# Row sums for the input's norm, inverse roots spread by transfers, and another order on ScalarE

## The chip, the core and the metric

The program runs on one core of a Trainium2 chip, in one launch. The metric is the device time of that launch in microseconds (us). The core has a matrix engine (TensorE, "PE" in the profile, its weight loads "PEld"), three engines for elementwise work (VectorE "DVE", ScalarE "ACT", GpSimd "POOL"), and SyncE ("SP"), which here issues all transfers. The engines run their own instruction streams and meet at semaphores. Data lie in SBUF (128 partitions), matmuls write to PSUM banks, and larger data lie in the chip's memory (HBM).

## The reference

Two transformer layers over x of shape (16, 256, 256): 16 batch entries, 256 positions, 256 features. Layer 0, cut to what matters:

```python
def _tc_rmsnorm(x, t, gw, gb, bw, bb):
    g = (t @ gw.T + gb)[:, None, :]
    b = (t @ bw.T + bb)[:, None, :]
    inv_rms = jax.lax.rsqrt(jnp.mean(x * x, axis=-1, keepdims=True) + EPS)
    return g * x * inv_rms + b
# layer 0 (inside), with 16 heads of 16
z = x + _attention(_tc_rmsnorm(x, t, g1w, g1b, b1w, b1b), Wq, Wk, Wv, Wo)
y0 = z + _swiglu(_tc_rmsnorm(z, t, g2w, g2b, b2w, b2b), gate_w, hid_w, out_w)   # hidden size 1024
x1 = x + y0
# layer 1: masked attention of x1, then
out = out @ Wo.T
rms = jnp.sqrt(jnp.mean(out * out, axis=-1, keepdims=True) + EPS)
xn = out / rms * rms_scale
xn = xn * (1.0 + sc[:, None, :]) + shift[:, None, :]
result = x1 + xn
```

So there are three norms with a root per position: of the input (layer 0 only, "N"), of the attention's output with the residual (layer 0, "C"), and of the attention's output (layer 1, "C" and then "R"). The mask keeps the first so many key positions for all rows. In layer 1 the kernel takes a short path in which one half of the keys is skipped; the profiled execution takes it.

## The kernel before

Everything is kept transposed: features on partitions, positions along the free dimension, so a batch entry is a tile of 128 x (2 x 256). Matrix products are made of three matmuls on split operands (a high part and a low part, `mm3`, lines 525 to 527), which is why so many "high" and "low" tiles appear.

The work is a pipeline over 32 items: 16 batch entries in layer 0 and the same 16 in layer 1. A step s works on several items at once (`stages`): N of item s+3 (its norm and split), A of s+2 (Q and K projections), V and B1 of s+1 (value projection; scores for the row maxima), B2 of s (scores again, exponentials, half of the value product), C of s-1 (second half of the value product, division, output projection, squares for the norm), C2/C3 of s-2 and s-3 (SwiGLU, layer 0 only), R of s-2 (layer 1's norm applied and stored). Steps run from -3 to 33. Steps 2 to 12 have all of layer 0's stages, 13 to 16 have no N of layer 0 any more, 17 is the passage, and 18 to 29 are layer 1's; steps 30 to 33 empty the pipeline. Each step has eight slots g = 0..7, and the order on every engine is written out by hand: each engine's `step` walks the slots and issues its work there. No scheduler moves anything.

Two PSUM banks (`work0`, `work1`) are handed out in turn to all uses named in `bank_uses`: T1a, T1b, sh1, Q, T2, Wo, K, V, ms, sh0, F0 to F7, bcC, bcN. A use waits until the use two places before it in the list has been read. From step 19 on the small uses sh0, sh1 and bcR have a third bank, `acc`.

A norm before the change goes like this. Squares: on GpSimd, `nrm<-X` for the input in slot 2 (line 1280) and `dg<-y` for the output in slot 3 (line 1294). Mean squares: on TensorE with a column of 1/256 (`mean_squares`, line 710), slot 5 in layer 0, slot 6 in layer 1, into the bank "ms". VectorE adds epsilon (`rsqrt`, line 938), GpSimd raises to -0.5 (`inverse_roots`, line 1261). VectorE multiplies the roots into identity matrices (`diagonals`, line 945), TensorE multiplies these by ones, which puts the root of each position in every partition (`broadcast_rstd`, line 718; uses bcC, bcN in slot 6, bcR in slot 1 of the next step). VectorE then multiplies (`normalize`, line 951), reading the roots from PSUM. ScalarE applies gain and shift per partition (`affine`, line 1084) and casts the high part; GpSimd subtracts for the low part (`xnl`, line 1322, or `xcl`, line 1314), and TensorE's projections (Q and K of the next step wait for `n_lo`) or the SwiGLU's first product (waits for `c_lo`) use them. In slot 7 of layer 0 the output's affine pair and its cast stand on ScalarE ahead of the slot's exponentials `E<-s2ps` (line 1055), and the value product (`values`, line 622) at the next step's start waits for these.

Q and K are split in three bf16 parts: high on ScalarE, the rest on VectorE (`rest`, line 919), middle on ScalarE (`middle`, line 1102), low on GpSimd (line 1233). SyncE writes the parts to a scratch tensor (`scr<-qp`, `scr<-kp`, line 412) and reads them back stacked along partitions (`read_stack`, line 422, `stack<-scr`), 768 KB per half of the heads; the scores of the next step read the stack. The attention's output is transposed in slot 2 (T2, line 670), ScalarE casts its high part (`oh`, line 1115), VectorE makes the low part (`ol`, line 909), and slot 3's output projection multiplies them.

SyncE's queue is in program order too: the x load, the shift rows of half 1, the writes of Q and K, `read_stack` of half 0, the store of a result (layer 1), the shift rows of half 0, `read_stack` of half 1. A wait in it holds everything behind it.

At the start, GpSimd also sets constant rows of the stacks (`stack_constants`, six memsets), in slot 3 of the first step, and SyncE loads the weights, 1 MB each.

## Time and profile before

| | us |
|---|---|
| median of 3 runs | 1011.88 |
| lowest, highest | 1011.34, 1016.07 |
| the profiled execution, its own time | 1008.46 |
| its span, first to last instruction | 1006.6 |
| TensorE busy | 909.2 (90%) |
| VectorE busy | 570.3 (57%) |
| ScalarE busy | 547.5 (54%) |
| GpSimd busy | 415.2 (41%) |
| transfers, mean share of the 16 engines | 39.8% |

The busy shares are means over very different stretches. The start, until about 100 us, fills the pipeline; layer 0 runs until about 740 us, with one full step every 39.6 us; layer 1 runs to about 960; the rest empties the pipeline. The 40 slices of the page show TensorE at nine tenths or more from slice 5 to slice 29 and at eight in layer 1; transfers take two to three tenths in layer 0 and five to seven in layer 1. A timeline row gives the start, the length, the engine, the line and the operation; what is in brackets at its end is the idle time before it and the instruction whose end ended it. A matmul group's length holds a modelled tail of about 0.16 that overlaps with the next group.

### The profile page before, as it was taken

The page shows a single profiled execution, that of the slowest core. Times are in us where ns is not written, and L with a number is a line of the kernel's source. Part 1 is how long each engine was busy: PE and PEld are TensorE (multiplying, and loading weights), DVE is VectorE, ACT ScalarE, POOL GpSimd, SP SyncE. Part 2 cuts the span into 40 slices and gives each one's busy share as a digit, 9 for nine tenths or more (in the row PEclk, how much of TensorE's full clock was granted, in tenths as well). Part 3 has the DMA queues.
Part 4 walks back from the last instruction along what each step waited for, and adds up shares of the span by engine and source line. Part 5 has one row for each costly group of instructions (what it writes and reads, how often), then busy time and mean ns, then how long its engine had stood idle before and what let it go on. Part 6 is the DMA issues. An engine that isn't in the chain of part 4 may idle for free.

```text
span 1006.6 us, 24326 instructions
## 1 busy us (share of the span) xinstructions
PE 909.2 (90%) x8188; PEld 780.6 (78%) x8188; DVE 570.3 (57%) x1104; ACT 547.5 (54%) x1130; POOL 415.2 (41%) x633
## 2 busy tenths in 40 slices
PE   3578899999999999999999999999999789888874
PEld 3456698898888988988889889889887677777653
DVE  3366556557555565575565756545455455555541
ACT  2246556546455565464554665554556566666652
POOL 5223344443443444434334344344444454444522
PEclk9779999999999999999999999999999999999997
DMA  6555423322332233223322242232437576576611
GB/s 204 110 106 122 91 64 75 75 65 59 66 86 42 63 73 73 63 58 68 84 42 63 69 91 65 65 76 66 94 74 167 119 160 147 142 166 144 157 36 34
DMA packets 83070, 91.29 MB, mean 91 GB/s; under 512 B 7776, under 2 KB 70016, under 8 KB 83008
## 3 DMA queue, kind: packets, MB, share of 16 engines
q1 hardware_dynamic: 83008, 90.50, 39.8%
q8 instruction: 35, 0.57, 0.3%
q14 instruction: 27, 0.22, 0.1%
HBM read 60.30 MB, written 29.36 MB: 89 GB/s over the span
## 4 chain that ended last, share of the span: by engine, by line
PE 73%; issue 8%; DVE 7%; ACT 5%; POOL 3%; DMA 1%; SPq 1%; POOLq 0%; DVEq 0%; ACTq 0%
PE work L525 11%; PE work L527 11%; PE work L526 11%; PE pvps L622 8%; PE s2ps L606 7%; PE s1ps L583 5%; PE work L710 4%; PE acc L525 3%; PE acc L526 2%; PE acc L527 2%; PE work L656 2%; PE s1ps L568 2%; PE work L718 1%; DVE rest L919 1%; DVE th L959 1%
## 5 line engine op out<-in xcount | busy, mean ns | idle before, releaser
L1055 ACT ACTIVATE E<-s2ps 128x512 f32<-128x512 f32 x384 | 214.1, 596 | 184.2 <-PE s2ps L606 110.8
L882 DVE TENSOR_REDUCE nmax<-s1ps 128x2 f32<-128x512 f32 x256 | 163.9, 682 | 32.1 <-PE s1ps L583 31.9
L525 PE MATMUL work<-xch,Gh 128*128 128x256 f32 x512 | 154.5, 302 | 0.0
L959 DVE SCALAR_TENSOR_TENSOR th<-th,work 128x256 f32<-128x256 f32 x128 | 53.8, 420 | 168.7 <-ACT th L1073 168.7
L1328 POOL TENSOR_TENSOR hl<-hf,hh 128x256 fp32r<-128x256 f32 x128 | 94.9, 742 | 131.0 <-PE acc L527 77.3
L526 PE MATMUL work<-xcl,Gh 128*128 128x256 f32 x512 | 147.1, 287 | 0.0
L527 PE MATMUL work<-xch,Gl 128*128 128x256 f32 x512 | 146.9, 287 | 0.0
L606 PE MATMUL s2ps<-stack 100*128 100x256 bf16 x768 | 127.7, 275 | 2.1 <-DMA stack<-rows 2.0
L875 DVE TENSOR_REDUCE nmax<-s1ps 128x4 f32<-128x512 f32 x128 | 85.6, 685 | 36.5 <-PE s1ps L568 36.4
L525 PEld LDWEIGHTS work<-xch,Gh 128*128 128x128 f32 x512 | 99.3, 194 | 8.2 <-issue 6.6
L622 PE MATMUL pvps<-E,vaug 128*32 128x256 f32 x1536 | 97.5, 387 | 6.3 <-ACT E L1055 4.0
L1233 POOL TENSOR_TENSOR qp<-rest,qp 128x512 bf16<-128x512 f32 x32 | 37.2, 1163 | 156.3 <-ACT qp L1102 156.3
L527 PEld LDWEIGHTS work<-xch,Gl 128*128 128x128 f32 x512 | 100.0, 195 | 0.0
L526 PEld LDWEIGHTS work<-xcl,Gh 128*128 128x128 f32 x512 | 99.9, 195 | 0.0
L583 PE MATMUL s1ps<-stack 96*128 96x256 bf16 x512 | 81.9, 281 | 9.4 <-DMA stack<-scr 4.9
L1073 ACT ACTIVATE th<-work 128x256 f32<-128x256 f32 x128 | 49.1, 384 | 72.3 <-PE work L527 72.3
L525 PE MATMUL work<-xnh,Wh 128*128 128x256 f32 x256 | 79.3, 310 | 1.4 <-issue 0.8
L606 PEld LDWEIGHTS s2ps<-stack 100*128 100x128 bf16 x768 | 67.3, 98 | 14.1 <-issue 2.3
L622 PEld LDWEIGHTS pvps<-E,vaug 128*32 128x32 f32 x1536 | 43.8, 110 | 40.3 <-issue 9.5
L525 PE MATMUL acc<-hh,Uh 128*128 128x256 f32 x256 | 74.2, 290 | 0.2
L526 PE MATMUL work<-xnl,Wh 128*128 128x256 f32 x256 | 74.4, 291 | 0.0
L527 PE MATMUL work<-xnh,Wl 128*128 128x256 f32 x256 | 74.2, 290 | 0.0
(131 smaller groups left out, 2149.1 us busy)
## 6 DMA issues: line engine op xcount, KB each, us to landing
stack<-scr SPq DMA_DIRECT2D x64, 384.0 KB, 4.6
stack<-scr SPq DMA_DIRECT2D x64, 256.0 KB, 5.2
scr<-qp SPq DMA_DIRECT2D x64, 192.0 KB, 2.3
scr<-kp SPq DMA_DIRECT2D x64, 192.0 KB, 2.3
stack<-scr SPq DMA_DIRECT2D x64, 128.0 KB, 5.6
X<-xT SPq DMA_DIRECT2D x16, 256.0 KB, 4.5
yT<-crm SPq DMA_DIRECT2D x16, 256.0 KB, 5.2
stack<-rows SPq DMA_DIRECT2D x196, 4.0 KB
```

Of the source, the lines that this page charges most:

```text
L525: mm(out, lh, rh, start=first, stop=False, skip_group_check=True)
L526: mm(out, lh, rl, start=False, stop=False, skip_group_check=True)
L527: return mm(out, ll, rh, start=False, stop=last, skip_group_check=True)
L583: last = mm(bank[:, T * i:T * (i + 1)], qst[par][0:PARTS, h, P * qh:P * (qh + 1)], kst[par][0:PARTS, h, :], start=st.L["B1"] == 0, stop=Tr ...
L606: last = mm(bank[:, T * i:T * (i + 1)], kst[par][0:ROWS, h, P * kh:P * (kh + 1)], qst[par][0:ROWS, h, :], start=not add_mask, stop=True, s ...
L622: last = mm(pvps[32 * i:32 * (i + 1), T * (j % 2):T * (j % 2 + 1)], v_of[:, kh, h, :], E[:, exp_slot(layer, st.full, h // 2, kh), T * (h % ...
L875: v.tensor_reduce(nmax[:, g // 4, :, 2 * (g % 4):2 * (g % 4) + 2], s1ps[g % 2][:, :].rearrange("p (q h t) -> p q h t", q=2, h=2), AX_X, AL ...
L882: v.tensor_reduce(nmax[:, g // 4, qh, 2 * (g % 4):2 * (g % 4) + 2], s1ps[u % 2][:, :].rearrange("p (h t) -> p h t", h=2), AX_X, ALU.max, n ...
L959: v.scalar_tensor_tensor(th[:, i % 2, :], th[:, i % 2, :], 1.0, bank[:, 0:T], ALU.add, ALU.mult).then_inc(silu_ready, 1)
L1055: a.activation(E[:, exp_slot(st.L["B2"], st.full, g, kh), :], s2ps[g % 2 if short else u % 2][:, :], ACT.Exp, scale=SCORE_SCALE).then_inc( ...
L1073: a.activation(th[:, i % 2, :], bank[:, 0:T], ACT.Tanh, scale=0.5).then_inc(tanh_ready, 1)
L1328: p.tensor_tensor(hl[:, i % 2, :], hf[:, i % 2, :], hh[:, i % 2, :].bitcast(F32), ALU.subtract).then_inc(h_low, 1)
```

## The change

It does five things.

1. Input's norm: the row sums. The input is also given by rows (`x_rows`: positions on partitions). SyncE loads that tile into `nrm`, ScalarE squares it in slot 3 with a scale of 1/16, and VectorE sums it along the free dimension. GpSimd's squares and TensorE's mean squares of the input go.
2. The slot. In steps with layer-0 work, `mean_squares` (output only), the variances and the roots are in slot 4 (was 5). In layer 1 they stay in slot 6.
3. Spreading. `diagonals` and `broadcast_rstd` go, with the bank uses bcR, bcC and bcN. SyncE writes the 2 or 4 roots of each partition to a small tensor in HBM, waits for the landing, and reads the whole of it back into every partition of `dg`. In layer-0 steps this stands behind `read_stack` of half 0 and ahead of the shift rows of half 0; in layer 1 behind these rows and ahead of `read_stack` of half 1. `normalize_c` and `normalize_n` read `dg` with a step of 4 or 2 elements.
4. ScalarE in layer-1 steps: the middle part of K moves from the end of slot 1 to slot 2, behind `oh` and the slot's exponentials.
5. The start: the input rows are the first load; ScalarE waits for the conditioning (`cond_ready`) only in slot 7 of the first step; GpSimd's `stack_constants` move from slot 3 to the first step's end, behind `xnl`.

```diff
-        return 5
+        return 4
     return None if L["C"] is None else 6
+def norm_columns(L):
+    return 0 if L["N"] == 0 else 2, 4 if L["C"] is not None else 2
...
-        if g == 1 and L["R"] is not None:
-            uses.append("bcR")
-        if g == 6:
-            uses += ["bcC"] * (L["C"] == 0) + ["bcN"] * (L["N"] == 0)
...
+        r_scr = nc.dram_tensor("r_scr", (P, 4), F32, kind="Internal").ap()
...
+            def load_rows(n):
+                sp.dma_start(flat(nrm[:, :, :]), x_rows[:, bass.ds(n * TC * D, TC * D)]).then_inc(rows_loaded, 16)
+            load_rows(0)
             load_x(0)
...
+                def spread_roots():
+                    c0, c1 = norm_columns(L)
+                    after(sp, rstd_spread, spread_before)
+                    after(sp, rstd_ready, roots_made)
+                    k = c1 - c0
+                    sp.dma_start(bass.AP(r_scr.tensor, 0, [[k, P], [1, k]]), rstd[:, c0:c1]).then_inc(rstd_written, 16)
+                    after(sp, rstd_written, roots_written)
+                    sp.dma_start(flat(dg[:, c0:c1, :]),
+                                 bass.AP(r_scr.tensor, 0, [[0, P], [1, k * P]])).then_inc(rstd_spread, 16)
...
                 if L["B2"] is not None:
                     rows_in(1)
+                if L["N"] == 0 and st.s0 > FIRST:
+                    after(sp, n_lo, split_before)
+                    load_rows(n_x)
...
                 load_swap(6)
+                if norm_slot(L) == 4:
+                    spread_roots()
                 if L["R"] is not None:
                     store_result(st.n(-2 - B), result_made)
                 if L["B1"] is not None:
                     rows_in(0)
+                if norm_slot(L) == 6:
+                    spread_roots()
...
-                if st.L["N"] == 0:
-                    after(pe, sq_n, st.n(3) + 1)
-                    jobs.append((nrm[:, :, :], 0))
...
-            def broadcast_rstd(st, use, col):
-                bank, full = open_bank(st, use)
-                after(pe, diag_ready, st.n(2 if use == "bcR" else 3) + 1)
-                mm(bank[:, 0:T], ones[:, :], dg[:, col:col + 2, :].rearrange("p a b -> p (a b)"),
-                   start=True, stop=True).then_inc(full, 1)
...
+            def variances(st):
+                if st.L["N"] == 0:
+                    n = st.n(3)
+                    after(dve, sq_n, n + 1)
+                    v.tensor_reduce(sums[:, :], nrm[:, :, :], AX_X, ALU.add).then_inc(sums_ready, 1)
+                    after(dve, sums_ready, n + 1)
+                    v.tensor_scalar(var[:, 0:2], sums[:, :], EPS, VAR_TOP, ALU.add, ALU.min).then_inc(var_ready, 1)
+                if st.L["C"] is not None:
+                    bank, free = opened(st, "ms")
+                    v.tensor_scalar(var[:, 2:4], bank[:, 0:2], EPS, VAR_TOP, ALU.add, ALU.min).then_inc(free, 1)
+            def spread(made, col):
+                c0, c1 = norm_columns(made.L)
+                after(dve, rstd_spread, 16 * (made.n(3) + 1))
+                by_row = flat(dg[:, c0:c1, :]).rearrange("q (p c) -> q c p", c=c1 - c0)
+                return by_row[:, col - c0:col - c0 + 2, :][:, None, :, :].to_broadcast([P, FC, TC, P])
+            def normalize_c(made):
+                v.tensor_tensor(halves(crm[:, :, :]), halves(y[:, :, :]), spread(made, 2), ALU.mult).then_inc(c_normed, 1)
...
+                    if g == 2 and L["A"] == 1:
+                        middle(st, "K", kp, k_mid)
                     if g == 2 and L["R"] is not None:
...
+                    if g == 3 and L["N"] == 0:
+                        n = st.n(3)
+                        after(act, rows_loaded, 16 * (n + 1))
+                        a.activation(nrm[:, :, :], nrm[:, :, :], ACT.Square, scale=D ** -0.5).then_inc(sq_n, 1)
...
-                    if g == q_slot(L, 1):
+                    if g == 2 and L["A"] == 0:
                         middle(st, "K", kp, k_mid)
...
-                    if g == 3 and st.s0 == FIRST:
-                        pool.wait_ge(sq_n, 1)
-                        for i in range(2):
-                            stack_constants(i)
-                        pool.wait_ge(stack_ones, 6)
...
+                if st.s0 == FIRST:
+                    pool.wait_ge(n_lo, 1)
+                    for i in range(2):
+                        stack_constants(i)
+                    pool.wait_ge(stack_ones, 6)
```

GpSimd's queue in the first two steps, before (`xnl` is the input's low part, `qp` and `kp` the low parts of Q and K, line 1280 the input's squares):

```order
16 L1280 TENSOR_TENSOR nrm<-X 128x512
17 L1225 MEMSET stack 4x2048
18 L1226 MEMSET stack 1x2048
19 L1228 MEMSET stack 1x2048
20 L1225 MEMSET stack 4x2048
21 L1226 MEMSET stack 1x2048
22 L1228 MEMSET stack 1x2048
23 L1261 TENSOR_TENSOR rstd<-var,power 128x2
24 L1322 TENSOR_TENSOR xnl<-nrm,xnh 128x512
25 L1233 TENSOR_TENSOR qp<-rest,qp 128x512
```

and the same place after the change:

```order
16 L1280 TENSOR_TENSOR rstd<-var,power 128x2
17 L1328 TENSOR_TENSOR xnl<-nrm,xnh 128x512
18 L1240 MEMSET stack 4x2048
19 L1241 MEMSET stack 1x2048
20 L1243 MEMSET stack 1x2048
21 L1240 MEMSET stack 4x2048
22 L1241 MEMSET stack 1x2048
23 L1243 MEMSET stack 1x2048
24 L1248 TENSOR_TENSOR qp<-rest,qp 128x512
25 L1248 TENSOR_TENSOR kp<-rest,kp 128x512
```

The memsets stood ahead of the roots and now stand between `xnl` and the first Q's low part.

ScalarE's queue in a layer-1 step, slots 1 to 3, before (`kp<-work` is K's high part, `kp<-rest` its middle part, `oh` the output's high part):

```order
775 L1146 CAST kp<-work 128x512
776 L1102 CAST kp<-rest 128x512
777 L198 REGISTER_ALU
778 L1115 CAST oh<-work 128x512
779 L198 REGISTER_ALU
780 L1055 ACTIVATE E<-s2ps 128x512
```

and after:

```order
780 L1156 CAST kp<-work 128x512
781 L1126 CAST oh<-work 128x512
782 L199 REGISTER_ALU
783 L1068 ACTIVATE E<-s2ps 128x512
784 L199 REGISTER_ALU
785 L1068 ACTIVATE E<-s2ps 128x512
786 L1115 CAST kp<-rest 128x512
```

The middle part moved behind `oh` and the exponentials; of the two rows of exponentials there, an execution on the short path runs one.

TensorE's queue between slot 6 and slot 7 of a full layer-0 step, before (`acc` is the SwiGLU's second product):

```order
931 L527 MATMUL acc<-hh,Ul 128x256
932 L198 REGISTER_ALU
933 L718 MATMUL work<-dg,ones 128x256 x2
934 L198 REGISTER_ALU
935 L583 MATMUL s1ps<-stack 128x256 x2
```

and after:

```order
915 L556 MATMUL acc<-hh,Ul 128x256
916 L199 REGISTER_ALU
917 L612 MATMUL s1ps<-stack 128x256 x2
```

The two broadcasts between them are gone.

## Rows read from the trace of the kernel before

**Rows 1.** stages by window: us, then busy (xinstructions) of each engine, clock, DMA.

```profile
200.00:300.00 100.00, 98.59 (x886) 88.44 (x888) 62.87 (x120) 52.81 (x115) 40.62 (x59) 0.98 0.30 67
800.00:900.00 100.00, 88.12 (x866) 71.75 (x865) 55.44 (x112) 66.09 (x127) 48.28 (x79) 0.98 0.65 146
```

**Rows 2.** TensorE's timeline, one layer-0 step: start us, us, engine, line, operation [idle before].

```profile
423.15 0.95 PE L710 MATMUL work<-mean,nrm 128*128 128x1 f32 x8
...
432.05 0.70 PE L718 MATMUL work<-dg,ones 128*128 128x256 f32 x2 [0.23 <-DVE hf L963]
...
435.71 0.64 PE L622 MATMUL pvps<-E,vaug 128*32 128x256 f32 x8
```

**Rows 3.** ScalarE's timeline, the same stretch.

```profile
432.78 1.09 ACT L1084 ACTIVATE crm<-crm,cond 128x256 f32<-128x256 f32 x2 [1.41 <-DVE crm L951]
...
434.43 1.08 ACT L1055 ACTIVATE E<-s2ps 128x512 f32<-128x512 f32 x2
```

**Rows 4.** VectorE's timeline, the same stretch.

```profile
431.91 0.68 DVE L951 TENSOR_TENSOR crm<-y,work 128x512 f32<-128x512 f32 x1
```

**Rows 5.** GpSimd's timeline, the same stretch.

```profile
431.45 0.73 POOL L1328 TENSOR_TENSOR hl<-hf,hh 128x256 fp32r<-128x256 f32 x1 [2.27 <-PE acc L527]
```

**Rows 6.** VectorE's timeline at 758 us.

```profile
758.57 0.42 DVE L945 TENSOR_TENSOR dg<-ident,rstd 128x256 f32<-128x256 f32 x1
```

**Rows 7.** GpSimd's timeline at 758 us.

```profile
758.74 0.33 POOL L1247 TENSOR_TENSOR nparts<-nmax,units 128x16 bf16<-128x16 f32 x1 [0.94 <-DVE nmax L889]
759.14 0.22 POOL L1249 TENSOR_TENSOR nrest<-nmax,nparts 128x16 f32<-128x16 f32 x1
```

**Rows 8.** VectorE's timeline, a layer-1 step at 855 us.

```profile
854.97 0.69 DVE L919 TENSOR_TENSOR rest<-work,kp 128x512 f32<-128x512 f32 x1 [1.38 <-ACT kp L1146]
856.90 0.69 DVE L909 TENSOR_TENSOR ol<-work,oh 128x512 fp32r<-128x512 f32 x1 [1.24 <-ACT oh L1115]
```

**Rows 9.** ScalarE's timeline, the same stretch.

```profile
855.69 0.62 ACT L1102 CAST kp<-rest 128x512 bf16<-128x512 f32 x1 [0.81 <-DVE rest L919]
856.21 0.58 ACT L1115 CAST oh<-work 128x512 fp32r<-128x512 f32 x1
```

**Rows 10.** TensorE's timeline in layer 1.

```profile
857.64 0.38 PE L525 MATMUL work<-oh,Wh 128*128 128x256 f32 x1 [1.63 <-DVE ol L909]
...
879.12 0.40 PE L568 MATMUL s1ps<-stack 97*128 97x128 bf16 x4
```

**Rows 11.** SyncE's DMA issues in layer 1.

```profile
867.38 1.38 SPq L422 DMA_DIRECT2D stack<-scr  x3
```

**Rows 12.** GpSimd's timeline at the start.

```profile
4.62 1.80 POOL L1225 MEMSET stack<- 4x2048 f32 x1
...
13.38 1.80 POOL L1228 MEMSET stack<- 1x2048 f32 x1
...
25.06 1.26 POOL L1322 TENSOR_TENSOR xnl<-nrm,xnh 128x512 fp32r<-128x512 f32 x1 [8.32 <-ACT xnh L1179]
31.47 1.16 POOL L1233 TENSOR_TENSOR qp<-rest,qp 128x512 bf16<-128x512 f32 x1 [5.15 <-ACT qp L1102]
```

**Rows 13.** TensorE's timeline at the start.

```profile
44.87 1.04 PE L583 MATMUL s1ps<-stack 96*128 96x256 bf16 x4 [4.90 <-DMA stack<-scr]
...
47.12 0.56 PE L525 MATMUL work<-xnh,Wh 128*128 128x256 f32 x1
```

**Rows 14.** time to landing of the transfers that L385 issues.

```profile
DMA to landing us min/median/max: 2.7/4.5/8.7
```

**Rows 15.** time to landing of the transfers that L412 issues.

```profile
DMA to landing us min/median/max: 2.1/2.3/4.6
```

**Rows 16.** GpSimd's and VectorE's timeline at the end.

```profile
997.78 0.71 POOL L1261 TENSOR_TENSOR rstd<-var,power 128x2 f32<-128x2 f32 x1 [1.45 <-DVE var L938]
...
1000.39 0.69 DVE L951 TENSOR_TENSOR crm<-y,acc 128x512 f32<-128x512 f32 x1 [1.44 <-PE acc L718]
```

More of the change, by code:

```diff
@@ L141, in turns_of @@
     uses = bank_uses(stages(s))
-    small = [u for u in uses if s >= SPARE and u in ("sh0", "sh1", "bcR")]
+    small = [u for u in uses if s >= SPARE and u in ("sh0", "sh1")]
     return [u for u in uses if u not in small], small
@@ L763, in step @@
                             divide_out(st)
-                    if g == ms_slot(L):
+                    if g == norm_slot(L) and L["C"] is not None:
                         mean_squares(st)
@@ L1256, in inverse_roots @@
             def inverse_roots(st):
[L1258 to L1260 removed]
+                c = slice(*norm_columns(st.L))
+                if st.L["N"] == 0:
+                    after(pool, var_ready, st.n(3) + 1)
+                if st.L["C"] is not None:
+                    b, k = st.bank("ms")
+                    after(pool, work_free[b], k + 1)
+                after(pool, rstd_written, 16 * st.n(3))
                 p.tensor_tensor(rstd[:, c], var[:, c], power[:, c], ALU.pow).then_inc(rstd_ready, 1)
@@ L1289, in step @@
                         after(pool, work_free[b], k + 1)
-                        b, k = st.bank("bcR") if L["R"] is not None else \
-                            st.last().bank("bcN" if st.last().L["N"] == 0 else "bcC")
-                        after(pool, work_full[b], k + 1)
+                        after(pool, c_normed, st.n(-1))
                         p.tensor_tensor(dg[:, :, :].rearrange("p (c u) t -> p c (u t)", c=FC),
```

103 lines of the change are left out of this document (36 added, 67 removed).

## The prediction

> **What bounds the kernel now.** I read the stages by window first, then each engine's timeline through one step of each kind, then the start and the end. In layer 0's steady part TensorE is busy 98.6 of 100 us, so an instruction taken from it is time, provided nobody else becomes late. In layer 1 it is busy 88.1 of 100 us, so there a chain with gaps sets the pace [rows 1]. The gap is one wait per step: TensorE stands 1.63 us in front of the output projection, for `ol` [rows 10]. In the first 100 us the pipeline is filling: every step waits for a chain through several engines, and nothing hides an added transfer. So I price the start, the eleven full layer-0 steps, the twelve layer-1 steps and the end apart. I price the four mixed steps between (13 to 16) in a sentence.
>
> **Layer 0, steps 2 to 12.** The mean squares of the input leave TensorE: 0.84 us, half of the block whose first half starts at 423.15 and reads 0.95 with its modelled end [rows 2]. The two broadcasts leave too. The second starts at 432.05 after waiting for VectorE to free its bank, and lasts 0.70 with its tail [rows 2]. Together with the first one and that wait TensorE would be free about 1.4 us earlier in slot 7. Most of that is not to be had. Its next long work, the value product at 435.71 [rows 2], needs the last exponentials. These stand on ScalarE behind the two affine instructions of the output's norm (432.78) and a cast, and end at 434.43 + 1.08 = 435.51 [rows 3]. That chain hangs on VectorE's normalize at 431.91 [rows 4], which program order puts behind the sixth slot's SwiGLU, and none of it used the removed matmuls in a way that delays it. So the broadcasts give only the slack 435.71 - 435.51 = 0.20. Sum so far: 0.84 + 0.20 = 1.04 per step.
>
> What hides the replacement: the mean squares move a slot forward, where the squares are ready over a microsecond earlier. ScalarE's square (about 0.6, as a cast of 512 columns, 0.62 in [rows 9]) and VectorE's sum (0.68, as any 512-column pass, [rows 4]) fall into idle time ahead of slot 4's work. The roots are then ready about 5 us earlier than now, and two transfers of 2.3 us [rows 15] fit ahead of 431.9. I cost them at nothing; without the cover it would be up to 4.6.
>
> Two things make the normalize itself later, and it is on the chain. First, its multiplier now comes from SBUF, not PSUM, so it reads two SBUF operands. The trace shows what such an instruction does to GpSimd: while VectorE's `dg<-ident,rstd`, also with two SBUF operands, runs from 758.57 to 758.99 [rows 6], GpSimd's first shift operation, started at 758.74, takes 0.33 and ends 0.08 after it, while its sister takes 0.22 [rows 7]. I take this as one waiting for the other. In the layer-0 step GpSimd's `hl` runs from 431.45 to 432.18 [rows 5], across 431.91, so the normalize starts 0.27 later. The Trainium skill (SBUF — State Buffer, Summary: rules for kernel authors) says that when VectorE has two SBUF inputs and GpSimd reads SBUF, the second to issue is fully blocked; by that rule, the trace agrees.
>
> Second, with four roots per row the multiplier is read with a step of 16 bytes. No row shows such a read. The bounds are 0.68, the present duration at unit step [rows 4], and twice that, 1.36, if each element took two turns. I take 0.98, so 0.30 more, with 0 and 0.68 kept for the range. Per step: 1.04 - 0.27 - 0.30 = 0.47; eleven steps give 5.2 us (bounds 1.0 and 8.5). The four mixed steps lose a broadcast, keep the slack of 0.20 each, and have only two roots per row: 0.8 us.
>
> **Layer 1, steps 18 to 29.** ScalarE now does the middle part of K (855.69, 0.62), then `oh` (856.21, 0.58) [rows 9]; VectorE's `ol` follows at 856.90 and TensorE at 857.64 [rows 8, 10]. With `oh` first it runs directly after the high part of K, ends near 855.5, and what is late next is VectorE itself: K's rest ends at 854.97 + 0.69 = 855.66 [rows 8], and `ol` starts behind it at 855.6. That is 1.3 earlier. TensorE must have the transposed output ready for this; it comes earlier too, as the broadcast that stood ahead of it is gone. Twelve steps: 15.6 us. The middle part of K slips by about 0.2 behind `oh` and one exponential, so GpSimd's low part, the K write and the stack read slip with it, and the step is shorter by 1.3. I take the first half of the stack read as still hidden. The roots' round trip sits on SyncE's queue ahead of the second half of the stack read (867.38 [rows 11]) and holds it for the write's landing, 2.3 [rows 15], and an issue of 0.4. Its last part is issued at 868.76 now and lands some 4.5 later, as a 256 KB load does [rows 14], at 873.3; it is needed at 879.12 [rows 10]. The 5.8 in hand become 5.8 - 2.7 - 1.3 = 1.8. So it costs nothing; rival 3 has the price if that fails.
>
> **The start.** Six memsets of the stacks, now from 4.62 to 15.18 in GpSimd's idle time [rows 12], move behind the first low part `xnl`. They last 13.38 + 1.80 - 4.62 = 10.56. `xnl` ends at 26.32 now [rows 12] and some 0.8 later then (one more load in front, one round trip behind a 1 MB load). So the memsets end near 37.7, and Q's low part, at 31.47 now [rows 12], is 6.2 late. K's low part follows it, then K's write and the stack read: the first scores move from 44.87 [rows 13] to 51.1. Worse, SyncE issues the roots' write behind that read. The queue serves in order as far as the trace tells: a 256 KB load lands in 4.5 as a rule and 8.7 behind two stack reads [rows 14]. So the roots are written at about 51.4, and read back 2.3 later [rows 15] at 53.8. From normalize to `xnl` it takes 0.7 + 1.1 + 0.6 + 1.3 and some hand-overs, 57.8. The next Q projection starts there instead of at 47.12 [rows 13]: +10.7. The next two steps put the roots' write behind a stack read again, at (8.7 - 4.5) / 2 = 2.1 each [rows 14]. Together 14.9 us later. Bounds: 8 if small writes overtake the stack reads, 17 if each round trip takes the longest landing.
>
> **The end.** The last group's roots (997.78 + 0.71 = 998.49) reach normalize at 1000.39 now, 1.9 later [rows 16]; with two transfers of 2.3 [rows 15] it is 4.7 later, so +2.8. Steps 30 and 31 save the 1.3 of the layer-1 step each: -2.6. Sum +0.2.
>
> **Sum.** 14.9 - 5.2 - 0.8 - 15.6 + 0.2 = -6.5 us. The profiled execution took 1008.46 us (span 1006.6), so 1002.0 by its own measure. The median of the runs, 1011.88, lies 3.4 above it: 1005.4.
>
> **Rivals.**
> 1. The start is cheap. If the small write overtakes the bulk reads, the start costs 8 and the sum is -13.4: 998.5. For it: the write is 128 tiny rows over all 16 engines. Against it: the 8.7 of [rows 14].
> 2. The strided read costs double, 1.36, on the chain of each of the eleven steps. Layer 0 then gives 1.04 - 0.27 - 0.68 = 0.09 per step, 1.0 us in all instead of 5.2: 1009.6, no change. For it: nothing in the rows has this step; against it: all rows of 512 columns on VectorE take 0.68 to 0.69, whatever they read. The Trainium skill (SBUF — State Buffer, Door 1: The DMA port swizzle) says that full rate needs two hits in a 16-byte line, and names four fp32 as the step that is still free. This read sits on that edge: one sentence of the page makes it slower, the other does not, and no row here decides.
> 3. Slower: the round trip turns layer 1 into a transfer-bound chain. SyncE waits on the roots' write before it may issue the second half of the stack read. If the write lands like the slowest of [rows 15], in 4.6, and the read-back ahead of that half takes another 1.6 from it, it is 2.3 + 1.6 = 3.9 later than I have it, with 1.8 in hand: twelve steps stand 2.1 us each in front of slot 4's scores, 25.2 us: 1005.4 + 25.2 = 1030.6. It decides from a landing of 2.3 + 1.8 = 4.1 us on. For it: transfers take 0.65 of the engines' time in layer 1 [rows 1]. Against it: at 867.38 the queue has just drained, and the medians are 2.3.
>
> **How the numbers follow.** Chances: forecast 0.42, rival 1 0.20, rival 2 0.26, rival 3 0.12. About 0.5% (5 us) is what a measurement can tell from no change. The forecast's own range, 999 to 1011, lies below 1006.8 in about 0.6 of cases and within 0.5% otherwise; rival 1 is faster; rival 2 is faster in 0.2, else the same, rarely slower; rival 3 is slower. Faster 0.42 x 0.62 + 0.20 + 0.26 x 0.2 = 0.51; slower 0.12 + 0.02 = 0.14; same 0.35. The range takes in rival 1 with a little more gain and rival 2 with the long start: 995 to 1015.
>
> **What would show it.** In layer 0 the normalize of the output (`crm<-y,dg`) shows the read's price, 0.68, 0.98 or 1.36, and TensorE an idle stretch of about a microsecond in front of the value product of the next step, released by the exponentials. In layer 1 TensorE's wait for `ol` falls from 1.63 to about 1, and the step is 1.3 shorter. The first Q projection after the first scores stands near 58 and the scores themselves near 51. Wrong would be: first scores still near 45 (the memsets don't hold Q's low part), TensorE waiting for `stack` in slot 4 of layer 1, or the broadcasts' full 1.4 us gained per layer-0 step, which would mean that the exponentials came earlier by another way.

## The result and the profile after

The changed kernel takes 1080.47 us (median of 4 runs, 1078.02 to 1082.12) against 1012.17 for the kernel before: 1.0665 times as long, 95% interval 1.0627 to 1.0702. I had predicted 1005.4. The profiled execution took 1082.12, its span is 1080.3.

The chain that ended last names the new thing at once (shares of the span, by engine and then by line):

```profile
PE 49%; DMA 17%; issue 14%; POOL 6%; ACT 5%; DVE 4%; SPq 4%; ACTq 0%; POOLq 0%; DVEq 0%
PE work L554 7%; PE work L556 7%; PE work L555 7%; PE pvps L651 6%; PE s2ps L635 5%; DMA stack<-rows 5%; DMA r_scr<-rstd 5%; PE s1ps L612 4%; DMA dg<-r_scr 3%; DMA stack<-scr 2%; PE work L733 2%; DMA scr<-kp 2%; PE work L685 2%; DVE crm L963 2%; PE acc L554 2%
```

Transfers hold 17% of it, the two of the round trip (`r_scr<-rstd`, `dg<-r_scr`) 8%. The windows of [rows 1], after the change (us, then busy of each engine, clock, DMA share):

```profile
200.00:300.00 100.00, 95.83 (x890) 86.41 (x889) 64.34 (x122) 55.99 (x123) 40.24 (x59) 1.00 0.38 85
800.00:900.00 100.00, 79.37 (x741) 64.28 (x740) 46.14 (x91) 56.01 (x108) 42.50 (x70) 0.91 0.64 139
```

Shares don't say where 74 us of span are. A ledger does: I took the start of one instruction that every step has, ScalarE's cast of K's high part, and subtracted (all in us; the last column is my forecast).

| stretch | before | after | change | forecast |
|---|---|---|---|---|
| start to K of step 2 | 129.8 | 166.8 | +37.0 | +14.9 |
| step 2 to 13 | 443.3 | 430.9 | -12.4 | -5.2 |
| 13 to 18 | 173.2 | 185.1 | +11.9 | -0.8 |
| 18 to 29 | 196.3 | 223.2 | +26.9 | -15.6 |
| 29 to the end | 64.0 | 74.3 | +10.3 | +0.2 |

**The start.** The chain of waits from 46 to 65 us (start, length, what), which answers to [rows 12, 13]:

```profile
46.40 2.33 DMA scr<-kp
...
50.17 5.15 DMA r_scr<-rstd
55.34 5.82 DMA dg<-r_scr
61.25 0.70 DVE nrm L967
...
65.11 0.58 PE work L554
```

A 1 KB write and its 128 KB read-back take 11.0 us. I had the write 0.3 behind the landing of the stack read and the read-back at 2.3. The first scores stand at 54.96, the Q projection behind them at 65.11. The two landings by stretch (median): in full layer-0 steps, where they are 2 KB and 256 KB, 2.4 and 3.2, in steps 13 to 16 3.3 and 4.1, in the start 5.1 and 4.0 (up to 6.6 and 5.8), in layer 1 4.5 and 5.1.

**Layer 0.** VectorE, ScalarE's exponentials and TensorE around the normalize, as in [rows 2 to 4]:

```profile
422.63 1.23 DVE L963 TENSOR_TENSOR crm<-y,dg 128x512 f32<-128x512 f32 x1
423.78 1.10 DVE L967 TENSOR_TENSOR nrm<-X,dg 128x512 f32<-128x512 f32 x1
...
425.70 1.08 ACT L1068 ACTIVATE E<-s2ps 128x512 f32<-128x512 f32 x2
...
426.90 1.93 PE L651 MATMUL pvps<-E,vaug 128*32 128x256 f32 x32 [1.76 <-ACT E L1068]
```

The value product waits 1.76 us for the exponentials, which hang on a normalize of 1.23 instead of 0.68. The period is 39.19 us; before it was 39.6 in six steps and 41.1 in five. In each of those five the granted clock is 0.96, so mostly 2.4 GHz and for a part of the time 1.2; after the change all eleven have 1.00. One of the five and one of the six, both of the kernel before:

```profile
248.70:289.90 41.20, 40.65 (x360) 36.41 (x358) 24.92 (x48) 22.06 (x49) 16.71 (x25) 0.96 0.30 65
331.00:370.60 39.60, 39.06 (x358) 34.83 (x357) 24.73 (x48) 21.91 (x49) 16.61 (x25) 1.00 0.32 67
```

TensorE's rows of the first one show where the clock falls:

```profile
262.54 1.03 PE L710 MATMUL work<-mean,dg 128*128 128x1 f32 x8
...
265.01 0.41 PE L527 MATMUL work<-xch,Gl 128*128 128x256 f32 x1
265.22 0.41 PE L525 MATMUL work<-xch,Gh 128*128 128x256 f32 x1
```

These matmuls start 0.21 apart, and from 268.1 on 0.12 again. In all five steps the fall comes 1.0 to 1.5 us behind the end of the sixteen 128x1 matmuls of the mean squares. The other six steps have the same sixteen and no fall.

**Steps 13 to 17.** Two rows of TensorE and one of GpSimd:

```profile
625.18 1.93 PE L651 MATMUL pvps<-E,vaug 128*32 128x256 f32 x32 [2.47 <-ACT E L1068]
...
641.13 0.39 PE L554 MATMUL acc<-hh,Uh 128*128 128x256 f32 x1 [1.96 <-POOL hl L1339]
```
```profile
639.24 1.15 POOL L1248 TENSOR_TENSOR kp<-rest,kp 128x512 bf16<-128x512 f32 x1 [7.55 <-ACT kp L1115]
```

In the first the round trip is late for the normalize. The second is new too: `hl` stands behind K's low part on GpSimd, and K's middle part moved behind the exponentials already in step 14, since Q and K of steps 14 to 17 belong to layer 1.

**Layer 1.** TensorE's waits of [rows 10] and SyncE's queue of [rows 11]:

```profile
920.13 0.39 PE L597 MATMUL s1ps<-stack 97*128 97x128 bf16 x4 [1.13 <-DMA stack<-scr]
923.11 0.39 PE L635 MATMUL s2ps<-stack 100*128 100x256 bf16 x2 [2.59 <-DMA stack<-rows]
...
930.22 0.39 PE L554 MATMUL work<-oh,Wh 128*128 128x256 f32 x1 [0.73 <-DVE ol L918]
```
```profile
913.33 1.27 SPq L432 DMA_DIRECT2D stack<-scr  x3
914.81 0.40 SPq L437 DMA_DIRECT2D yT<-crm  x1
915.32 2.04 SPq L481 DMA_DIRECT2D stack<-rows  x3
917.46 0.38 SPq L489 DMA_DIRECT2D r_scr<-rstd  x1
923.19 0.34 SPq L491 DMA_DIRECT2D dg<-r_scr  x1
923.57 1.38 SPq L432 DMA_DIRECT2D stack<-scr  x3
```

The wait for `ol` fell from 1.63 to 0.73, where I had named about 1. In its place are two waits for transfers, and SyncE issues the read-back 5.7 us behind the write, for whose landing it waits.

### The profile page after: what moved, and what is told of

It reads as the page before. It is cut to its first block, busy times and chain, and to the rows that moved or that the text cites. A ratio compares the mean times of both kernels' runs of the same rounds, so it can differ in the third digit from the quotient of the medians.

```text
span 1080.3 us, 23966 instructions
## 1 busy us (share of the span) xinstructions
PE 885.6 (82%) x7964; PEld 756.2 (70%) x7964; DVE 576.3 (53%) x1096; ACT 552.7 (51%) x1146; POOL 400.0 (37%) x617
## 4 chain that ended last, share of the span: by engine, by line
PE 49%; DMA 17%; issue 14%; POOL 6%; ACT 5%; DVE 4%; SPq 4%; ACTq 0%; POOLq 0%; DVEq 0%
PE work L554 7%; PE work L556 7%; PE work L555 7%; PE pvps L651 6%; PE s2ps L635 5%; DMA stack<-rows 5%; DMA r_scr<-rstd 5%; PE s1ps L612 4%; DMA dg<-r_scr 3%; DMA stack<-scr 2%; PE work L733 2%; DMA scr<-kp 2%; PE work L685 2%; DVE crm L963 2%; PE acc L554 2%
## 5 line engine op out<-in xcount | busy, mean ns | idle before, releaser
L635 PE MATMUL s2ps<-stack 100*128 100x256 bf16 x768 | 131.9, 281 | 19.5 <-DMA stack<-rows 18.8
L555 PE MATMUL work<-xcl,Gh 128*128 128x256 f32 x512 | 144.7, 283 | 0.0
L556 PE MATMUL work<-xch,Gl 128*128 128x256 f32 x512 | 144.4, 282 | 0.0
L976 DVE SCALAR_TENSOR_TENSOR th<-th,work 128x256 f32<-128x256 f32 x128 | 53.9, 421 | 168.1 <-ACT th L1086 168.0
L651 PE MATMUL pvps<-E,vaug 128*32 128x256 f32 x1536 | 100.0, 395 | 34.8 <-ACT E L1068 28.6
L612 PE MATMUL s1ps<-stack 96*128 96x256 bf16 x512 | 84.5, 286 | 45.1 <-DVE nmax L891 26.1
L556 PEld LDWEIGHTS work<-xch,Gl 128*128 128x128 f32 x512 | 97.5, 190 | 0.0
L555 PEld LDWEIGHTS work<-xcl,Gh 128*128 128x128 f32 x512 | 97.5, 190 | 0.0
L612 PEld LDWEIGHTS s1ps<-stack 96*128 96x128 bf16 x512 | 43.5, 102 | 66.7 <-issue 22.2
L554 PE MATMUL work<-xnh,Wh 128*128 128x256 f32 x256 | 82.9, 324 | 2.7 <-POOL xnl L1328 2.2
L1248 POOL TENSOR_TENSOR kp<-rest,kp 128x512 bf16<-128x512 f32 x32 | 40.4, 1262 | 120.2 <-ACT kp L1115 120.2
```

Source lines behind the costliest of these rows:

```text
L554: mm(out, lh, rh, start=first, stop=False, skip_group_check=True)
L555: mm(out, lh, rl, start=False, stop=False, skip_group_check=True)
L556: return mm(out, ll, rh, start=False, stop=last, skip_group_check=True)
L612: last = mm(bank[:, T * i:T * (i + 1)], qst[par][0:PARTS, h, P * qh:P * (qh + 1)], kst[par][0:PARTS, h, :], start=st.L["B1"] == 0, stop=Tr ...
L635: last = mm(bank[:, T * i:T * (i + 1)], kst[par][0:ROWS, h, P * kh:P * (kh + 1)], qst[par][0:ROWS, h, :], start=not add_mask, stop=True, s ...
L651: last = mm(pvps[32 * i:32 * (i + 1), T * (j % 2):T * (j % 2 + 1)], v_of[:, kh, h, :], E[:, exp_slot(layer, st.full, h // 2, kh), T * (h % ...
```

## The experiments

My first reading was that SyncE's wait for this landing makes layer 1 slow (rival 3 of the prediction), that the queue order makes the round trip slow at the start, and that part 4 gains a little. The kernels below went against most of that. Spans by the stretches of the ledger, us, one profiled execution each:

| kernel | to step 2 | 2-13 | 13-18 | 18-29 | rest | ratio to before (95%) |
|---|---|---|---|---|---|---|
| before | 129.8 | 443.3 | 173.2 | 196.3 | 64.0 | |
| after | 166.8 | 430.9 | 185.1 | 223.2 | 74.3 | 1.0665 (1.0627-1.0702) |
| mid_only | 132.0 | 443.2 | 182.0 | 213.8 | 69.0 | 1.0262 (1.0217-1.0308) |
| diag | 134.5 | 426.1 | 181.0 | 208.8 | 65.5 | 1.0104 (1.0063-1.0145) |
| late_read | 166.9 | 430.9 | 184.5 | 229.8 | 72.9 | 1.0635 (1.0588-1.0682) |
| consts_first | 162.7 | 430.9 | 186.4 | 223.0 | 76.8 | 1.0656 (1.0605-1.0708) |
| store_late | 130.5 | 443.2 | 182.0 | 192.9 | 67.2 | 1.0069 (1.0036-1.0102) |
| sums_only | 127.9 | 426.0 | 173.8 | 197.9 | 65.8 | 0.9788 (0.9739-0.9837) |
| spread_early | 161.5 | 430.9 | 185.8 | 222.8 | 74.3 | 1.0632 (1.0578-1.0685) |
| pool_write | 160.9 | 431.0 | 186.8 | 224.6 | 79.2 | 1.0665 (1.0611-1.0720) |
| thin_read | 168.0 | 430.9 | 185.0 | 214.2 | 73.3 | 1.0563 (1.0534-1.0591) |
| sums_store | 131.0 | 426.1 | 173.8 | 193.2 | 63.8 | 0.9781 (0.9748-0.9814) |
| sums_best | 128.3 | 426.1 | 173.8 | 190.9 | 63.7 | 0.9750 (0.9727-0.9772) |
| unit_step | 168.1 | 426.5 | 187.0 | 223.7 | 75.8 | 1.0665 (1.0590-1.0740) |

Kernels with the same instructions in a stretch agree there within 0.1 us in steps 2 to 13, but within some 3 us in the start and 5 in layer 1. So I read the small effects from the stretch or the step that they belong to.

### mid_only

```diff
+                    if g == 2 and L["A"] == 1:
+                        middle(st, "K", kp, k_mid)
...
-                    if g == q_slot(L, 1):
+                    if g == 2 and L["A"] == 0:
                         middle(st, "K", kp, k_mid)
```

> The kernel before with part 4 alone: K's middle part behind the output's high part and the exponentials, in every step whose Q and K projections belong to layer 1 (14 to 29). Theory: two effects. In the layer-1 steps TensorE's wait for ol falls from 1.63 to 0.7, as in the changed kernel's trace, so 12 x 0.9 = 11 us less. In steps 14 to 17 K's low part comes later and GpSimd's hl stands behind it; in the changed kernel TensorE waits 1.96, 1.98, 1.61 and 1.61 us there, so 7 us more. Sum -4: 1008. Rival A (the recorded prediction): only the gain, 1.3 per step, 996.6. Rival B: part 4 is what slows layer 1, 27 us more: above 1030.

1041.95 us: rival B. TensorE waits 1.95, 2.00, 1.62 and 1.61 for `hl` in steps 14 to 17, as in the changed kernel, and layer 1 takes 17.5 us more though the wait for `ol` is down to 0.5 per step. Its waits in layer 1, 780 to 960 us (total, times, longest), of before and of mid_only:

```profile
PE work L525 <- DVE ol L909: 16.0, 10, 1.6
...
PE s2ps L606 <- DMA stack<-rows: 1.7, 2, 1.5
PE s1ps L568 <- DMA stack<-scr: 1.2, 1, 1.2
```
```profile
PE s2ps L606 <- DMA stack<-rows: 12.1, 9, 1.6
PE s1ps L568 <- DMA stack<-scr: 5.4, 8, 0.8
PE work L525 <- DVE ol L909: 4.9, 9, 0.6
```

SyncE's queue tells why. First before, where the output projection of this step starts at 876.15, then mid_only, where it starts at 857.43:

```profile
876.14 0.89 SPq L412 DMA_DIRECT2D scr<-kp  x2
878.94 1.27 SPq L422 DMA_DIRECT2D stack<-scr  x3
880.42 0.41 SPq L427 DMA_DIRECT2D yT<-crm  x1
882.41 2.06 SPq L469 DMA_DIRECT2D stack<-rows  x3
```
```profile
858.93 0.89 SPq L412 DMA_DIRECT2D scr<-kp  x2
861.71 1.27 SPq L422 DMA_DIRECT2D stack<-scr  x3
863.20 0.41 SPq L427 DMA_DIRECT2D yT<-crm  x1
863.71 2.06 SPq L469 DMA_DIRECT2D stack<-rows  x3
```
```profile
868.26 0.39 PE L568 MATMUL s1ps<-stack 97*128 97x128 bf16 x4 [0.79 <-DMA stack<-scr]
869.97 0.39 PE L606 MATMUL s2ps<-stack 100*128 100x256 bf16 x2 [1.31 <-DMA stack<-rows]
```

Measured from the output projection, the first half of the stack read was issued at +2.8 and is now at +4.3, since TensorE has come nearer to K, not K to TensorE. It lands at +10.8, 6.55 after its issue, and TensorE is there 0.79 earlier. The shift rows are issued at +6.3 in both, but now 2.0 us behind the stack read and 0.5 behind the result's store instead of 3.5 and 2.0, and they land at +12.5; before, TensorE used them at +10.2 without a wait. The gain of 1.1 at `ol` is repaid by 2.1 in front of transfers. The granted clock falls with it, from 0.98 to 0.93 in 800:900, that is, more of this stretch runs at 1.2 instead of 2.4 GHz: after the waits of this step the projections' matmuls start 0.21 apart, elsewhere 0.12. Steps 18 to 29, before and in mid_only, show that this is the larger part:

```profile
746.28:942.59 196.31, 171.31 (x1701) 139.08 (x1700) 110.56 (x221) 127.08 (x242) 92.24 (x154) 0.99 0.66 149
757.28:971.10 213.82, 183.13 (x1701) 149.13 (x1700) 111.60 (x221) 127.05 (x243) 92.10 (x154) 0.93 0.60 137
```

The same 1701 matmuls keep TensorE busy for 11.8 us more, and it is idle for 5.7 more.

### diag

Part 3 undone: `diagonals`, `broadcast_rstd` and the uses bcR, bcC, bcN are back, `spread_roots` goes. All else stays as in the changed kernel.

> The changed kernel with part 3 undone: the roots go through identity matrices and a matmul with ones again (bank uses bcC, bcN, bcR), all the other parts stay. Theory: the spreading by transfers is nearly all of the 68 us. What stays is the memsets' shift at the start (+5.6, K's low part 5.6 later by them), 0.84 us less of TensorE per full layer-0 step (-9, and perhaps some us more where the granted clock rises), +7 in steps 14 to 17 and -11 in layer 1: 1012 + 5.6 - 9 + 7 - 11 = 1005, between 998 and 1012. Rival: the parts other than the spreading carry a good part of the loss (row sums behind a later load, part 4 in layer 1): 1030 or more.

1022.54 us. Against the changed kernel the start is 32.3 us shorter, layer 0 4.8, steps 13 to 18 4.1, layer 1 14.4 and the end 8.8: the spreading costs 58 us by the medians (1080.5 - 1022.5), 64 by the two profiled executions (diag's is the fastest of its six runs), and is the main cause. My number was too low, since it had part 4 as a gain; what is left over before, +7.8 in 13 to 18 and +12.5 in layer 1, is mid_only again. A full layer-0 step takes 38.73.

### late_read and thin_read

late_read, in layer-1 steps, and thin_read:

```diff
-                    after(sp, rstd_written, roots_written)
-                    sp.dma_start(flat(dg[:, c0:c1, :]), ...
...
                     read_stack(par, 1)
+                if norm_slot(L) == 6:
+                    read_roots()
```
```diff
-                    sp.dma_start(flat(dg[:, c0:c1, :]),
-                                 bass.AP(r_scr.tensor, 0, [[0, P], [1, k * P]])).then_inc(rstd_spread, 16)
+                    q = 16 if norm_slot(L) == 6 else P
+                    sp.dma_start(flat(dg[0:q, c0:c1, :]),
+                                 bass.AP(r_scr.tensor, 0, [[0, q], [1, k * P]])).then_inc(rstd_spread, 16)
```

> The changed kernel with one move on SyncE's queue, in layer-1 steps only: the wait for the roots' write and the read-back stand behind the second half of the stack read, not ahead of it. Theory: layer 1 is slow because SyncE stands 4.2 us per step (33.9 us in 8 waits) on the landing of a 1 KB write while the stack read waits behind it. Then the 11 steps from 782.7 to 1006.0 (223 us) fall to some 190 to 200, and the kernel to 1050 (1045 to 1058). Rival: the two extra transfers slow the others by sharing the engines, wherever they stand: 1075 to 1082.

> The changed kernel, but in layer-1 steps the roots are read back into 16 of the 128 partitions only (16 KB instead of 128 KB), so layer 1's norm is left out for the others. Theory: GpSimd's own queue and the later read-back did not bring layer 1's 14 us (against diag) back, since they left the volume; with an eighth of it the waits for the stack and the rows fall towards diag's (7.7 and 12.0 in ten steps), and the kernel takes 1068 to 1072. Rival: it is the number of transfers and the landings that count, not the volume: 1078 to 1082.

late_read: 1080.04, the rival. The second half of the stack read is issued 0.4 us behind the roots' write, not 6.1, and nothing comes of it. In steps 18 to 29 TensorE's wait for the stack falls from 16.6 to 11.3 us and its wait for the rows grows from 18.0 to 25.4, so rival 3 of my prediction had the sign right and the mechanism wrong. thin_read, whose layer-1 results are not the norm's: 1069.9, as expected, and layer 1 is 9.0 shorter in the ledger. Over these steps the two waits are 28.0 instead of 34.6 (diag 21.4), and TensorE's matmuls take 3.0 less, at a clock of 0.94 instead of 0.93. So the size of the read-back counts for more than half of the 14.4. Bytes and number of pieces both fell to an eighth, and no run separates them; the other 5 us, as much as the scatter of this stretch, stay open.

### consts_first

```diff
+                    if g == 3 and st.s0 == FIRST:
+                        pool.wait_ge(consts, 5)
+                        for i in range(2):
+                            stack_constants(i)
+                        pool.wait_ge(stack_ones, 6)
```

> The changed kernel with GpSimd's six memsets back ahead of the first roots. Theory: K's first low part comes at 39.2 instead of 44.8 and everything behind it 5.6 earlier, as the start is one chain from there to step 2: 1074.9. Rival: the chain is bound by SyncE's round trips and a weight load, and the 5.6 is lost again before step 2: 1079 to 1081.

1080.5, the rival's number. By the trace K's high part of step -1 comes 5.75 earlier, that of step 2 4.0. The memsets cost about what I had worked out (6.2 forecast), less what the later steps take back. In the total it is lost in the scatter of the later stretches.

### spread_early and pool_write

spread_early, then pool_write (on GpSimd behind the roots):

```diff
+                    if norm_slot(L) == 4 and st.s0 < 1:
+                        spread_roots()
                     after(sp, q_written, a_written)
```
```diff
+                after(pool, rstd_ready, st.n(3) + 1)
+                after(pool, rstd_spread, 16 * st.n(3))
+                p.tensor_tensor(spare[:, :], power[:, 0:1], power[:, 1:2], ALU.mult)
+                p.dma_start(bass.AP(r_scr.tensor, 0, [[k, P], [1, k]]), rstd[:, c]).then_inc(rstd_written, 16)
```

> The changed kernel with the roots' write and read-back, in steps -2, -1 and 0 only, ahead of the wait for the landing of K's write and so ahead of the first half of the stack read. Theory: at the start the write lands in 5.1 to 6.6 and the read-back in 3.9 to 5.8 because both queue behind 384 KB of stack read on the same queue. Ahead of it they take some 2.3 each and start 3 earlier where the roots are ready: about 8 us less in steps -2 and -1, some in step 0, K's high part of step 2 at 147 to 151, not 166.8: 1063. Rival: the transfers are slow there for the weight loads and for the kind of transfer (a read of 1 or 2 KB by each of 128 partitions): no more than 5 us less, 1076.

> The changed kernel with the roots' write issued by GpSimd on its own queue, directly behind the roots (with one small operation of 128x1 ahead of it that carries the wait); SyncE still waits for the landing and issues the read-back. Theory: the landing of 5.1 to 6.6 is the place behind the stack read on SyncE's queue, so on another queue it is 2.0 to 2.6 everywhere: 3 us less in each of the 4 steps of the start, layer 1 not faster by more than 5 as its bound is the stack read: 1066. Rival: the time goes by sharing the transfer engines with the read, whatever the queue: landings of 4 to 6 stay, 1080.

1076.5 and 1080.5, both the rival. Both bring 5 to 6 us at step 2. In spread_early, ahead of the stack read, the first of the moved writes takes 3.7 beside K's write and its read-back 5.3 beside the stack read. (The read is 768 KB in three transfers; the 384 KB of my theory is the first of them.) In pool_write the writes of steps -2, -1 and 0 go out ahead of the stack read and land in 5.0, 3.5 and 3.6 us (5.1, 6.6 and 6.0 in the changed kernel); their read-backs, now behind it, take 6.4, 7.1 and 6.2 (5.8, 3.9 and 4.0). What the writes gain the read-backs lose. The 5.0 is of a write with only K's write ahead of it and the stack read issued 1.6 us behind it, so what is issued soon after counts too.

The landings say more. In the changed kernel 29 of the 36 writes are issued while transfers issued earlier are still in flight, and 26 of them land 0.2 to 1.2 us behind the last of these (the stack read in layer 0, the result's store in layer 1), the other three 1.5 to 1.8. In full layer-0 steps they are issued 1.9 to 2.5 us before that read is through, hence the 2.0 to 2.7. The seven with nothing ahead of them (the shift rows aside, whose landing the profile doesn't give) take 2.7 to 3.9. In pool_write it is the same from the other queue: 0.2 to 0.3 behind the stack read in full layer-0 steps, 0.2 to 1.1 behind the store in layer 1. So in these traces the write waits for what was issued ahead of it, in whichever queue. The Trainium skill (DMA: Bandwidth & Descriptors, Issuing engines are not separate DMA queues) says that the issuing engines feed the same 16 transfer engines; the trace agrees, with these landings of GpSimd's write behind SyncE's transfers.

### store_late

```diff
-                if L["R"] is not None:
-                    store_result(st.n(-2 - B), result_made)
                 if L["B1"] is not None:
                     rows_in(0)
+                if L["R"] is not None:
+                    store_result(st.n(-2 - B), result_made)
```

> mid_only with the store of the result issued behind the shift rows of half 0, not between the first half of the stack read and these rows. Theory: layer 1 is now bound by the chain K's write, stack read, scores of the next step (K's write comes 1.5 us later relative to the output projection than before, the read of half 0 is used 5.8 to 6.4 us after its issue, not 7.3), and the rows queue behind the read and the 256 KB store. Without the store ahead of them the rows land about a microsecond earlier: TensorE's wait for them falls from 1.3 to below 0.5, its wait for the stack stays at 0.4 to 0.8, the step falls from 19.4 to some 18.4, the kernel from 1042 to 1031. Rival: the rows are late for another reason (the engines are busy with the stack read anyway): 1038 to 1042.

1019.78, 11 us less than expected: one 256 KB store behind 12 KB of rows takes 22 us off mid_only by the medians, 20 by the ratios (1.0069 against 1.0262). TensorE's waits, 780 to 960 us:

```profile
PE s1ps L568 <- DMA stack<-scr: 8.0, 10, 1.6
PE work L525 <- DVE ol L909: 5.5, 10, 0.6
...
PE s2ps L606 <- DMA stack<-rows: 3.0, 8, 0.7
```

The wait for the rows is 3.0 instead of 12.1, that for the stack 8.0 instead of 5.4, and the clock in 800:900 is 1.00 (0.98 before, 0.93 in mid_only). Steps 18 to 29:

```profile
755.77:948.65 192.88, 171.07 (x1701) 139.44 (x1700) 110.92 (x221) 126.95 (x243) 92.22 (x154) 0.99 0.67 151
```

Against mid_only that is 12.1 us less of the same matmuls and 8.9 less idle time. In mid_only's step above, the store lands at 868.81 and TensorE gets the rows at 869.97, 1.2 behind it; in store_late the store is not ahead of them. Layer 1 takes 192.9, less than before. So in layer 1 the rows' place behind the store is what made part 4 a loss; the stack read alone would not have. The 8.8 us in steps 13 to 18 stay.

### sums_only, sums_store and sums_best

sums_only is diag with K's middle part back in slot 1 and the memsets as in consts_first. sums_store adds store_late's edit. sums_best adds part 4 where R is not None:

```diff
+                    if g == 2 and L["A"] == 1 and L["R"] is not None:
+                        middle(st, "K", kp, k_mid)
...
-                    if g == q_slot(L, 1):
+                    if g == q_slot(L, 1) and L["R"] is None:
                         middle(st, "K", kp, k_mid)
```

> Parts 1 and 2 alone, so to say: the changed kernel with the spreading (3) and the move on ScalarE (4) undone, and the memsets (5) back ahead of the first roots. Theory: the start is that of before (K's high part of step 2 within 2 us of 129.8), full layer-0 steps take 38.73 as in diag (39.6 or 41.1 before), steps 14 to 29 are as before. By the ledger of K's high parts diag had gained 12.5 us at step 13 with the memsets' loss of 4.7 in it, so 17 without: 1012.2 - 17 = 995 (993 to 1000). Rival: with TensorE at over 96% in these steps the granted clock falls in some of them as it does before (0.96), and gives 1.5 us back in each: 1003.

> sums_only with the result's store behind the shift rows of half 0, as in store_late. Theory: with K's middle part in its old place TensorE waits for ol and not for a transfer in layer 1, so the order of two transfers moves nothing: within 3 us of sums_only, 991. Rival: the store delays the stack read or the rows even there: 986 or less.

> sums_store with part 4 in layer-1 steps only (18 to 29; K's middle part stays in slot 1 in steps 14 to 17, where GpSimd's hl would wait behind K's low part). Theory: with the store out of the way the output's high part ahead of K's middle part gives what store_late shows: the step is 17.2 on average, not 17.8, and no 1.6 to 2.0 is lost in steps 14 to 17: 11 x 0.5 = 5 us under sums_store, 986. Rival: the chain K's write, stack read, scores is as long as the step, so the gain at ol turns into a wait for the stack: 990 to 992.

990.96, 989.76 and 985.52 us: the first 2 us under the range that I gave, the other two as expected. Row sums and the earlier slot are worth 17 us by themselves in the ledger, all in steps 2 to 13 (22 by the medians). The 0.87 us per full step (39.6 to 38.73) are close to the 0.84 that I had for the mean squares; the five steps at 41.1 become 38.7 as well, with TensorE as busy as before:

```profile
200.00:300.00 100.00, 98.91 (x905) 88.48 (x903) 63.62 (x124) 57.04 (x126) 40.41 (x59) 1.00 0.33 77
```

In steps 14 to 17 sums_best has none of mid_only's loss (173.8 against 182.0). Part 4 with the store moved gives 2.3 us in steps 18 to 29, 4.2 in the medians; both are within the scatter, and the intervals of the two kernels overlap. sums_best has the lowest median of all, 2.5% under before.

### unit_step

```diff
-                by_row = flat(dg[:, c0:c1, :]).rearrange("q (p c) -> q c p", c=c1 - c0)
+                by_row = flat(dg[:, c0:c1, :]).rearrange("q (c p) -> q c p", c=c1 - c0)
```

> The changed kernel in which the normalizes read dg at unit step, 128 neighbouring elements for each half, and not with a step of 4 or 2. The layout of the roots is as it was, so they multiply by other positions' roots: the values are not the norm's, the work is the same. Theory: the 16-byte step costs crm<-y,dg 1.23 instead of 0.68 and nrm<-X,dg 1.10 instead of 0.69 in full layer-0 steps, and the first stands on the chain to the exponentials and the value product. At unit step both take 0.68 to 0.70, TensorE's idle time in front of the value product falls from 1.76 to 1.2, and the step from 39.19 to 38.7: 11 x 0.5 = 5.5 us less, 1075. Rival: what makes these two longer is GpSimd's traffic or the second SBUF operand, not the step: durations and period stay, 1080.

```profile
382.79 0.82 DVE L963 TENSOR_TENSOR crm<-y,dg 128x512 f32<-128x512 f32 x1
383.53 0.68 DVE L967 TENSOR_TENSOR nrm<-X,dg 128x512 f32<-128x512 f32 x1
...
386.66 1.93 PE L651 MATMUL pvps<-E,vaug 128*32 128x256 f32 x32 [1.35 <-ACT E L1068]
```

The normalizes are 0.41 and 0.42 shorter (1.23 and 1.10 before), TensorE's wait is 0.41 shorter, and the step is 38.79, 0.40 shorter: 4.4 us over the stretch. The 0.14 that `crm<-y,dg` keeps over 0.68 goes with GpSimd's `hl`, which runs for the first 0.28 of it; `nrm<-X,dg`, also with two SBUF operands but with GpSimd idle, takes 0.68. The total did not move, 1081.11: the start and steps 13 to 18 came out 1.3 and 1.9 longer. A layout by column, which would keep the values right at unit step, has no time on record.

## Why the prediction was wrong, step by step

- **The start, +14.9; measured +37.0.** The memsets were right, and so was the write's place behind the stack read: it landed 0.4 behind it where I had 0.3, so it does not overtake and rival 1 is out. Two steps failed. The first is "some 0.8 later then": that had the first round trip, beside a 1 MB load, as nearly free, and it took 10.5 (5.1 and 5.3), so `xnl` ends at 31.35 instead of 27.1 and the first scores stand at 54.96 instead of 51.1. The second is "read back 2.3 later [rows 15]": I priced a 128 KB read into 128 partitions by a write to HBM, and it took 5.8. So the Q projection stands at 65.11 instead of 57.8. For the later steps I added 2.1 twice, and the round trip takes 10.2 to 11.1 us in each of the first four norms. diag shows the cost of the spreading in the start as 32.3. The upper bound of 17 came from the same rows and was no bound.
- **Layer 0, 0.47 per step; measured 0.40.** The mechanism held. TensorE idles in front of the value product, released by the exponentials. The 16-byte step costs 0.41 where I took 0.30 of 0 to 0.68, the block 0.14 where I took 0.27: the normalize started with `hl` still running and was not held for the whole overlap. The broadcasts gave about 0.1, where I took 0.20: unit_step's 38.79, with the block's 0.14 in it, is 0.06 over diag's 38.73. That the sum comes so near is in part errors that cancel. On the step the Trainium skill (SBUF — State Buffer, Door 1: The DMA port swizzle) counts four fp32 as free; 1.10 against 0.68 says that it is not, while the step of two elements in layer 1 is, at 0.68. What I did not see is a granted clock of 0.96 in five of eleven steps of before, which make them 41.1 and not the 39.6 that I gave for every full step. It was in the windows, had I asked by step and not by 100 us; its end gave another 7.5 us.
- **Steps 13 to 16, -0.8; measured +11.9 up to step 18.** Failed twice. I read part 4 as a change of steps 18 to 29, but its condition holds from step 14 on; the `hl` waits are 7.2 us. And "keep the slack of 0.20 each" forgot that the round trip ends on the same chain: 2.47, 1.26 and 1.72 in front of the value product.
- **Layer 1, -15.6; measured +26.9.** The wait for `ol` fell to 0.73, near the forecast of about 1. The failing step is "I take the first half of the stack read as still hidden": I checked the second half (5.8 in hand) and not the first, and not the rows behind it. mid_only gives +17.5 for this, two thirds of it through the lower clock, and store_late its mechanism. The other failing step is "So it costs nothing" of the round trip: diag gives it 14.4, with 34.6 us of TensorE's waits for rows and stack against 21.4. The write landed in 4.5 (median), not 2.3, behind the result's store. Rival 3 was on the right side, but its mechanism, the held second half, fell with late_read.
- **The end, +0.2; measured +10.3.** The last trip takes 6.9 us from the roots to the normalize (before 1.9, forecast 4.7). diag puts 8.8 of it on the spreading.

## What to carry to other kernels

A wait that a change removes was also cover: list every transfer that the next step needs, with its issue, its landing and its first use, not only the one nearest to the edit. Price a new round trip by a transfer of its own kind with the same traffic in flight, and where no row has that, let the bound reach to the slowest landing seen for a transfer in such a place, times the steps in which nothing hides it. And evaluate each new condition for every step of the pipeline; the mixed steps are where an edit for one layer acts in the other.

## What was new about the hardware

- A write of 1 or 2 KB landed 0.2 to 1.2 us behind the last transfer issued ahead of it in 26 of 29 cases, from SyncE's queue, and the same way behind SyncE's transfers from GpSimd's. With nothing ahead it took 2.7 to 3.9 us, directly behind a stack read of 768 KB up to 6.6.
- Order among small and large transfers on one queue matters at the scale of a whole layer: 12 KB behind or ahead of a 256 KB store is some 20 us over some 16 steps (mid_only against store_late).
- TensorE at 98.6% busy was granted 0.98 in the kernel before (0.96 in five steps) and 1.00 at 98.9% with the mean squares' 128x1 matmuls halved (sums_only). The kernels with sixteen of them in a block (before, mid_only, store_late) lose it in the same five steps, 1.0 to 1.5 us behind the block in before; all the kernels with eight lose it in none. Why these five and not the other six is not shown, and no run halves the block alone.
- In layer 1 short waits and the granted clock go together: 0.93 in mid_only, 1.00 in store_late (800:900), and 183.1 against 171.1 us of TensorE for the same 1701 matmuls. No run shows which comes first.
